# Negated softmax maxima carried as three rows of the query stack in a fused two-attention, two-MoE kernel

## What is computed

```
q = (x @ Wq).reshape(B, S, 32, 8)        # 32 query heads of 8
k = (x @ Wk).reshape(B, S, 8, 8)         # 8 key/value heads, repeated 4 times
v = (x @ Wv).reshape(B, S, 8, 8)
q, k = rope(q), rope(k)
scores = einsum('bhqd,bhkd->bhqk', q, k) / sqrt(8)
scores = where(causal, scores, neg)
probs = softmax(scores, axis=-1)
out = einsum('bhqk,bhkd->bhqd', probs, v)
out = out.transpose(0, 2, 1, 3).reshape(B, S, 256) @ Wo
```

## Time and profile before

| | us |
|---|---|
| median of 3 runs | 918.64 (917.73 to 919.67) |
| the profiled execution | 916.41 |
| its span, first to last instruction | 914.2 |
| PE busy | 791.1 (87%) |
| DVE busy | 365.2 (40%) |
| ACT busy | 290.5 (32%) |
| POOL busy | 224.3 (25%) |

### The profile page before, as it was taken

One profiled execution on the slowest core, in us unless ns is written; L12 is line 12 of the kernel. 1 busy time (PEld: TensorE's weight loads), 2 busy tenths in 40 slices (PEclk: granted clock), 3 DMA queues, 4 the chain that ended last, 5 costly groups with the idle time before them and its releaser, 6 DMA issues.

```text
span 914.2 us, 14814 instructions
## 1 busy us (share of the span) xinstructions
PE 791.1 (87%) x5020; PEld 602.4 (66%) x5021; DVE 365.2 (40%) x902; ACT 290.5 (32%) x527; POOL 224.3 (25%) x260
## 2 busy tenths in 40 slices
PE   1989799999989999999955289989887999999990
PEld 0767577877767677777734257767665767777760
DVE  8444154543533312222146386676543422222212
ACT  1102103114233333433223214445453234334321
POOL 8341013333131411221123300011312421221212
PEclk9999899999999999999986789999998999999995
DMA  6963914223962216110221641211301111101004
GB/s 198 409 142 107 315 67 93 59 48 89 360 207 74 70 55 207 40 35 23 63 78 32 177 103 34 56 45 35 142 30 53 58 36 34 34 24 34 29 18 143
DMA packets 47692, 88.19 MB, mean 96 GB/s; under 512 B 8884, under 2 KB 36916, under 8 KB 45524
## 3 DMA queue, kind: packets, MB, share of 16 engines
q1 hardware_dynamic: 36104, 54.56, 21.0%
q0 software_dynamic: 7568, 30.97, 9.3%
q10 hardware_dynamic: 3968, 1.97, 0.8%
HBM read 52.33 MB, written 35.13 MB: 96 GB/s over the span
## 4 chain that ended last, share of the span: by engine, by line
PE 80%; DVE 8%; DMA 6%; issue 2%; ACT 2%; POOL 1%; SPq 0%; ACTq 0%; POOLq 0%; DVEq 0%
PE bank L1380 24%; PE bank L1407 13%; PE bank L880 9%; PE bank L459 4%; PE bank L504 4%; PE bank L1393 4%; PE bank L515 2%; PE bank L449 2%; PE bank L533 2%; PE bank L502 2%; PE bank L576 2%; DMA PTR<-rows_out 2%; DVE stat L324 2%; DVE XN L596 1%; PE bank L550 1%
## 5 line engine op out<-in xcount | busy, mean ns | idle before, releaser
L1380 PE MATMUL bank<-wgu,R 128*128 x736 | 225.4, 459 | 0.4 <-issue 0.3
L1380 PEld LDWEIGHTS bank<-wgu,R 128*128 128x128 f32 x736 | 137.7, 193 | 65.8 <-issue 3.5
L1407 PE MATMUL bank<-R 112*128 (+1 forms) x552 | 127.0, 379 | 1.2 <-ACT R L1429 1.2
L1407 PEld LDWEIGHTS bank<-R 112*128 112x128 f32 (+1 forms) x552 | 104.4, 190 | 22.3 <-issue 1.7
L1445 DVE TENSOR_TENSOR R<-R,bank 128x344 f32<-128x344 f32 x92 | 47.2, 513 | 179.9 <-PE bank L1380 172.2
L647 ACT ACTIVATE PTR<-bank 128x512 f32<-128x512 f32 x144 | 83.5, 597 | 97.7 <-PE bank L504 82.2
L1356 POOL DMA_INDIRECT rows_out<-R,XN x46 | 46.0, 999 | 169.4 <-ACT R L1437 157.7
L1452 DVE COPY R<-bank 112x512 f32<-112x512 f32 x46 | 31.7, 690 | 103.7 <-PE bank L1393 103.7
L596 DVE TENSOR_REDUCE XN<-bank 128x2 f32<-128x512 f32 x96 | 63.1, 684 | 10.7 <-PE bank L459 10.7
L1423 ACT ACTIVATE R<-bank 128x344 f32<-128x344 f32 x92 | 41.9, 457 | 76.4 <-PE bank L1380 76.2
L1437 ACT ACTIVATE R<-bank 128x256 f32<-128x256 f32 x46 | 17.7, 384 | 146.7 <-PE bank L1407 146.7
(11 more groups left out here) (167 smaller groups left out, 1292.0 us busy)
## 6 DMA issues: line engine op xcount, KB each, us to landing
wgu<-in_wgu SPq DMA_DIRECT2D x10, 1376.0 KB, 11.4
slots_in<-PTR POOLq DMA_DIRECT2D x1, 9088.0 KB, 26.1
row_of_slot<-in_unused POOLq DMA_DIRECT2D x2, 4544.0 KB, 17.6
R<-slots_in SPq DMA_DIRECT2D x46, 128.0 KB, 2.0
wgu<-R SPq DMA_DIRECT2D x32, 128.0 KB, 2.4
R<-R SPq DMA_DIRECT2D x32, 128.0 KB, 2.4
PTR<-rows_out SPq DMA_DIRECT2D x16, 256.0 KB, 3.1
R<-in_wd SPq DMA_DIRECT2D x8, 448.0 KB, 5.8
```

The lines of the kernel that those rows point to most:

```text
L1380: last = nc.tensor.matmul(BK[2 * half + gu][:, 0:IH], xsT[:, p, kk, :], wgu[:, bass.ds(e * (KD * GU) + (kk * GU + gu * I + half * IH), IH) ...
L1407: last = nc.tensor.matmul(down_bank(i)[:, 0:D], hT[0:CH[c], p, c, :], wd[0:CH[c], bass.ds(e * (6 * D) + c * D, D)], start=c == 0, stop=c == 5)
```

## The change

In the second attention the eight extra matmuls of each group, which add the negated maxima, are dropped. The three parts of the maxima become rows 72, 73 and 74 of the query stack, which face rows of ones in the key stack, so that the key-query product adds them itself. The stacks are used with 72 rows for the scores and with 75 for the shifted scores. After the copy into `nTs`, ACT waits for its own copy and issues three DMAs per batch, one per part: 32 rows of `nTs` (32 heads by 256 bf16, 16 KB) go to one partition of `qsb`. The semaphore `max_e` counts 49 per batch (SHIFT_B: one for the copy, 16 for each DMA), and both of its waits on PE want the full count. Since the transfers take time, the maxima are made one iteration earlier: `scores_in` puts two groups at g = 1 and none at g = 6, and the transposition and copy move from g = 7 to g = 6. The memsets now fill rows of the key stack alone, with ones. The first attention keeps its matmuls.

```diff
-            return (GB, (lambda h: qsb[b % 2][:, h, :]), (lambda h: ksb[b % 2][:, h // 4, :]), (lambda h: h // 4), HDB,
-                    SCALE_B, wob)
+            return (GB, (lambda h: qsb[b % 2][0:rows, h, :]), (lambda h: ksb[b % 2][0:rows, h // 4, :]), (lambda h: h // 4),
+                    HDB, SCALE_B, wob)
...
                     if i == 2 and g == 0:
-                        later(nc.tensor, s["max_e"], b)
+                        later(nc.tensor, s["max_e"], SHIFT_B * b)
...
-            G, q, k, v, hd, scale, wo = heads(l, b)
+            G, q, k, v, hd, scale, wo = heads(l, b, RB + PARTS)
             bank, nT = banks(l, g, True), nTs[b % 2]
             if g == 0:
-                nc.tensor.wait_ge(s["max_e"], b + 1)
+                nc.tensor.wait_ge(s["max_e"], (SHIFT_B if l == 2 else 1) * (b + 1))
...
-                    nc.tensor.matmul(bank[i][:, j * S:(j + 1) * S], sel[:, h:h + 1].broadcast_to([PARTS * 32, P]),
-                                     nT[:, :], start=False, stop=False, skip_group_check=True)
+                    if l == 0:
+                        nc.tensor.matmul(bank[i][:, j * S:(j + 1) * S], sel[:, h:h + 1].broadcast_to([PARTS * 32, P]),
+                                         nT[:, :], start=False, stop=False, skip_group_check=True)
...
+            if l == 2:
+                nc.scalar.wait_ge(s["max_e"], SHIFT_B * b + 1)
+                for n in range(PARTS):
+                    nc.scalar.dma_start(qsb[b % 2][RB + n:RB + n + 1, :, :],
+                                        nTs[b % 2][32 * n:32 * n + 32, :]).then_inc(s["max_e"], 16)
...
+        SHIFT_B = 16 * PARTS + 1
...
-            if b >= B or g == GB - 1:
+            if b >= B or g >= GB - 2:
                 return []
-            return [(b, 0), (b, 1)] if g == 0 else [(b, g + 1)]
+            return [(b, 2 * g), (b, 2 * g + 1)] if g < 2 else [(b, g + 2)]
...
-                if g == GB - 1 and b < B - 1:
+                if g == GB - 2 and b < B - 1:
                     max_tensor(2, b + 1)
...
-            nc.gpsimd.memset(heads_b[1][64:RBZ, :], 0.0).then_inc(s["zeroed"], 1)
+            nc.gpsimd.memset(ksb[1][64:RBZ, :, :], 1.0).then_inc(s["zeroed"], 1)
...
-            dve.memset(heads_b[0][64:RBZ, :], 0.0).then_inc(PB["zeroed"], 1)
+            dve.memset(ksb[0][64:RBZ, :, :], 1.0).then_inc(PB["zeroed"], 1)
```

More of the change, by code:

```diff
@@ L393, in norm_scalar, with heads @@
                     evac_scalar(l, b - 1)
-        def heads(l, b=0):
+        def heads(l, b=0, rows=RB):
             if l == 0:
                 return GA, (lambda h: qst[b % 2][:, h, :]), (lambda h: kst[b % 2][:, h, :]), (lambda h: h), HDA, SCALE_A, woa
-            return (GB, (lambda h: qsb[b % 2][:, h, :]), (lambda h: ksb[b % 2][:, h // 4, :]), (lambda h: h // 4), HDB,
-                    SCALE_B, wob)
+            return (GB, (lambda h: qsb[b % 2][0:rows, h, :]), (lambda h: ksb[b % 2][0:rows, h // 4, :]), (lambda h: h // 4),
+                    HDB, SCALE_B, wob)
         def values_of(l, b):
@@ L512, in shifted_tensor @@
                 h = 4 * g + j
-                nc.tensor.matmul(bank[2][:, j * P:(j + 1) * P], sel[:, h:h + 1].broadcast_to([PARTS * 32, P]),
-                                 nT[:, P:S], start=False, stop=False, skip_group_check=True)
+                if l == 0:
+                    nc.tensor.matmul(bank[2][:, j * P:(j + 1) * P], sel[:, h:h + 1].broadcast_to([PARTS * 32, P]),
+                                     nT[:, P:S], start=False, stop=False, skip_group_check=True)
                 last = nc.tensor.matmul(bank[2][:, j * P:(j + 1) * P], k(h)[:, P:S], q(h)[:, P:S],
```

## The result

The changed kernel took 935.46 us (median of 4 runs, 928.22 to 939.6), the kernel before 918.58 beside it: a ratio of 1.018, 95% interval 1.0146 to 1.0213. The prediction was 912.6, range 907 to 918.5, with a chance of 0.08 for slower. It was slower by 17 us, and 23 us above the forecast. The profiled run took 936.49 us, span 934.3, 20.1 us more than the span of 914.2 before.

The account below looks back on a forecast made before the run. PE was taken to set the pace in the attention's iterations. Terms of 16.6 - 0.4 - 4.2 - 4.3 - 1.7 gave 6.0 us gained, from a median of 918.64 to 912.6 us, range 907 to 918.5.

Parts of the forecast that it names:

- What bounds the kernel: Second attention's iterations: PE sets the pace at 4.03 us without a gap, so removing a matmul shortens them, though not everywhere.
- term 1: Second attention, all batches: the removed matmuls save 0.66 us per counted group, 16.6 us together; fewer contracted rows cost nothing.
- The rival that DVE takes over the pace: Attention iterations: full ones stay at 3.7 instead of 3.37 us, losing 5 us, 917.6 us in all; chance 0.06.
- Term 2: Iteration g = 1: two groups of scores, made earlier, make PE wait for DVE's maxima; -0.4 us in all.
- Term 3: Start of the attention: PE waits for three DMAs, L = 3.6 us from first issue to last landing; -4.2 us, clock included.
- Term 4: Three later batch boundaries: PE waits 1.3, 1.3 and 1.7 us more for the transfers, with L = 3.6; -4.3 us.
- Term 5: Gaps at g = 4 and ahead of batch 3: one fall to half clock, 3.4 us long; -1.7 us.
- The rival of other traffic: Three later boundaries: SP's loads, issued alongside, delay ACT's transfers to L = 8.2; 926.4 us; chance 0.07.
- Iterations of 3.37: Sign: batch 0 iterations with one scores group take 3.37 us.
- Shifted scores 3.6 + 0.65 behind the first issue: Sign at the start: the first shifted scores come 3.6 + 0.65 us behind the first DMA issue.
- Gaps of 1.3, 1.3 and 2.1: Sign: PE gaps of 1.3 us ahead of the third scores bank at two boundaries, about 2.1 ahead of batch 3.
- The gap at g = 4 at 2.1: Sign: PE's wait for DVE at the layernorm of g = 4 grows from 1.45 to 2.1 us.

Follow-up runs that it names:

- b4: Kernel before in its own order, but groups 2 to 7 take the maxima from the stack and groups 0 and 1 keep their matmuls: 916.0 us, ratio 0.9982.
- a2: Changed kernel without its twelve transfers and without subtracting the maxima, so not the reference's result: 906.2 us, ratio 0.9875 to the kernel before.
- a3: Kernel before with only the earlier order of scores and maxima, its matmuls kept and no transfer: 917.6 us, ratio 0.9976.
- b3: b1 with the three rows of a batch carried by one transfer in place of three: 918.0 us, ratio 1.0002 to the kernel before.
- a1: The changed kernel itself, measured again: 933.6 us, ratio 1.0155 to the kernel before.
- b1: a4 with SP also holding back the experts' first weights until the last boundary's transfers have landed: 918.4 us, ratio 1.0006 to the kernel before.
- b2: b1 plus 8, 8, 5 and 4 unread matmuls while PE waits for the landings of the four batches: 909.7 us, ratio 0.9920 to the kernel before.
- c4: Changed kernel with its long landings left, plus 14, 19, 19 and 4 unread matmuls in the waits: 926.2 us, ratio 1.0076 to the kernel before.
- c2: b2 plus, in later batches, 7 unread matmuls ahead of the norm's transpositions and 3 ahead of the ranks: 910.9 us, ratio 0.9923 to the kernel before.
- c3: c2's order and filling, but group 0 of each batch keeps its matmuls with the maxima: 911.8 us, ratio 0.9917 to the kernel before.
- a4: Changed kernel with the second half of SP's stack reload held back until ACT's three transfers have landed: 925.7 us, ratio 1.0052 to the kernel before.
- c1: Kernel before plus unread matmuls where its PE waits (4 at the start; 5 and 2 in later batches): 921.0 us, ratio 1.0020.

## Why the prediction was wrong

**What bounds the kernel, and term 1 (16.6 us): right.** PE sets the pace in the iterations; 4.03 became 3.37 us to the last digit, and at full clock 75 rows cost what 96 do; whether they cost something through the clock is open (see b4). Over the attention a2 has 14.7 us for terms 1 and 2 together, for 16.2. The rival that DVE takes over the pace is ruled out by the same 3.37.

**Term 2 (-0.4): wrong sign, small.** a3 has about +2, with an interval of 0.4 to 4.

**Term 3 (-4.2): right but for its clock.** From the first transposition to the first shifted scores the start went from 1.26 to 551.49 - 546.36 = 5.13 us, 3.87 more against 3.85; L was 3.4 to 3.5 for 3.6. By the estimate from the Trainium skill, "SBUF — State Buffer", section on the DMA port swizzle, it would have been 3.8. b3, with all 48 KB in one transfer, measured 3.76 to 3.95, which agrees. The 0.3 us for the clock belongs to term 5.

**Term 4 (-4.3): the first failed step.** It took L = 3.6, the value for a quiet queue, at all four places. At the boundaries L was 6.9 and 6.6 (a1: 6.2 and 6.1), and at the last 3.5 or 8.0, by whether SP's weights were issued behind ACT's third row or ahead of it. With quiet queues (b1) PE waits 0.91, 0.96 and 0.99 for the 1.3, 1.3 and 2.15 of the term, so its working was sound, if a little high, and its input was not. I had the case as a rival, with the right mechanism and place, and gave it 0.07, on the ground that the 7.28 us landing of the earlier trace rows was another kind of transfer. The ground was no evidence on the question: SP's issues at the batch ends were in the trace, and they meet the transfers, since both stand at the end of the batch. The price of this step, a1 against b1, each by its distance to the kernel before, is some 14 us, clock included.

**Term 5 (-1.7): the second failed step.** It counted one fall of the clock among the gaps of the boundaries and of g = 4, and 0.3 us at the start. The trace has half clock for 7 to 9 us behind three of the four waits, and in b1, where these waits are short, still at the start and behind g = 4 (2.11 us, the growth of the earlier trace rows that the prediction foresaw). b1 less b2, 8.7 us, is what unread matmuls in the waits give back with quiet queues, against 2.0 charged for all of the clock. I had asked of each gap whether it was long enough to let the clock fall, and took the 3.4 us of the earlier trace rows for how long it then stays down. In b1 it stayed down for 13.5 us at the start, and in b4 for 17 with PE never idle. Why it stays down so much longer than before is not shown: the waits are a part of it (b2), the lower stacks may be another.

Both together: the forecast of 912.6 plus 6.7 (8.7 for the clock in place of 2.0) is 919.3, and b1 measured 918.4; plus 14 for the traffic is 933, and a1 measured 933.6. The rival of other traffic stood at 926.4. It had the mechanism, but took L as 8.2 at all three boundaries, where it was 6.9, 6.6 and 3.5, and had nothing for the clock. That c4, with this traffic and part of the clock held up, measured 926.2 is luck as far as the number goes.

**The signs named ahead.** Iterations of 3.37: seen. Shifted scores 3.6 + 0.65 behind the first issue: 4.2 (547.31 to 551.49). Gaps of 1.3, 1.3 and 2.1: 4.43, 4.18, 1.00. The gap at g = 4 at 2.1: 2.11. Batch 1 at 37.3 us: 45.7 (586.27 to 631.98), and 38.6 in b1. Half clock behind at most one gap: behind every long one. "Landings above 5 us, or half clock in every batch" were named as what would make it wrong; both came.

## What to carry to other kernels

A small transfer on the path has the length of its landing beside whatever the other queues do at that moment: look up in the trace who issues within a few microseconds of it, above all work released by the same event, and let the bulk loads wait for the small one. Before removing matmuls, ask which waits of PE grow by it: time that PE loses in a wait may be charged twice, once as the wait and once as the half clock behind it. A version that keeps the change, lets SP's loads wait and fills PE's waits (b2) is 0.8% below the kernel before (0.5 to 1.1%); c2 and c3 are level with it, and no version that computes everything is faster.

## What the runs showed of the hardware

- 16 KB into one SBUF partition, the last of three in a row on ACT's queue, landed 2.17 to 2.38 us behind its issue with SP quiet in most places (but 3.68 in b2 and 3.18 in c2 at the second middle boundary, cause open), 4.66 to 5.52 beside SP's reload of four loads, and 6.36 to 7.32 beside two weight loads.
- All 48 KB in one transfer took 3.76 to 3.95 us from its issue (b3), three transfers 3.4 to 3.6 from the first (b1).
- ACT's issue of one DMA, 0.51 to 0.61 us, was 1.65 us in one place of the first profile and 1.48 in a4 and 1.23 in c2, where SP's loads came only behind it, so it is not those that stretch it. I have no cause for it.
- 25 unread matmuls of 128x512, in waits of 2.60, 0.91, 0.96 and 0.99 us, were worth 8.7 us (b2 against b1), and 25 in the kernel before, whose clock was up already, -2.2 (c1).
- PE worked at half clock for 17 us with no idle time in them (b4), behind a wait of 2.36 us after which the kernel before had 3.4 us at half clock.
